# Boundary work between images regrouped, and one of three depthwise-convolution bands computed on VectorE

## The reference

```python
# layer 0
ll, lh, hl, hh = haar(x)                      # four 32x32 bands
q, k, v = heads(qkv_w @ ll)                   # 8 heads of 16, 1024 positions; q, k normalized
attn = softmax(keep_upper_half(q @ k.T / 4))  # each row keeps its 512 largest scores
ll_out = group_norm(proj_w @ (attn @ v))
y = silu(group_norm(depthwise3x3([lh, hl, hh])))      # 384 channels
high = [lh, hl, hh] + alpha * group_norm(pw_w @ y)
out = x + 0.1 * inverse_haar(ll + ll_out, high)
out = out + 0.1 * group_norm(w2 @ gelu(group_norm(w1 @ out)))
# layer 1: full attention over 4096 positions, one head of 16 for q and k
out = gamma * (Wo @ (V @ softmax(Q @ K.T / 4).T)) + out
```

## Time and profile before

| | |
|---|---|
| median of 3 runs | 6547.7 us (6547.65 to 6551.5) |
| profiled execution | 6551.84 us, of which the span of its instructions is 6550.0 us |
| busy share | TensorE 78%, VectorE 69%, ScalarE 70%, GpSimd 6% |
| mean granted TensorE clock | 0.886 |

### The profile page before, as it was taken

One profiled execution on the slowest core, in us unless ns is written; L12 is line 12 of the kernel. 1 busy time (PEld: TensorE's weight loads), 2 busy tenths in 40 slices (PEclk: granted clock), 3 DMA queues, 4 the chain that ended last, 5 costly groups with the idle time before them and its releaser, 6 DMA issues.

```text
span 6550.0 us, 92687 instructions
## 1 busy us (share of the span) xinstructions
PE 5096.8 (78%) x30756; PEld 3132.4 (48%) x30756; DVE 4551.3 (69%) x8207; ACT 4574.2 (70%) x6939; POOL 412.2 (6%) x135
## 2 busy tenths in 40 slices
PE   5343878876888868878788868887688778885788
PEld 2000445653666435553455435664356535563466
DVE  1676479954898469973898559974789649894443
ACT  3885389945998379954999369973799559993223
POOL 3000300011000200012000200003000110000000
PEclk8555889987999879998899879998799879997899
DMA  1001100011000110011000110001100120002000
GB/s 49 6 9 40 51 16 15 14 50 55 13 15 13 56 47 18 16 52 55 9 18 13 48 55 15 18 33 55 28 16 15 50 54 13 16 13 61 9 7 12
DMA packets 109767, 187.72 MB, mean 29 GB/s; under 512 B 48768, under 2 KB 53760, under 8 KB 106144
## 3 DMA queue, kind: packets, MB, share of 16 engines
q1 hardware_dynamic: 109216, 181.05, 9.1%
HBM read 110.61 MB, written 69.47 MB: 27 GB/s over the span
## 4 chain that ended last, share of the span: by engine, by line
DVE 33%; PE 25%; issue 19%; ACT 12%; DMA 5%; SPq 3%; POOL 2%; DVEq 1%; ACTq 0%; POOLq 0%
DVE MX L1400 9%; ACT work L891 7%; PE PS L493 6%; DVE arena L1378 6%; DVE M L1300 5%; PE PS L741 5%; PE PS L462 4%; DVE work L1292 3%; DVE work L1260 3%; DVE work L1284 2%; ACT work L909 2%; PE PS L434 2%; PE PS L405 2%; PE PS L645 2%; PE PS L480 1%
## 5 line engine op out<-in xcount | busy, mean ns | idle before, releaser
L891 ACT ACTIVATE work<-arena,T 128x1024 bf16<-128x1024 f32 x1792 | 2039.7, 1140 | 96.7 <-DVE T L1247 63.9
L493 PEld LDWEIGHTS PS<-V,work 128*128 128x128 f32 x16384 | 2011.1, 194 | 119.8 <-ACT work L916 29.1
L493 PE MATMUL PS<-V,work 128*128 128x129 f32 x16384 | 2040.1, 278 | 22.4 <-ACT work L916 22.4
L1400 DVE TENSOR_REDUCE MX<-PS 128x1 f32<-128x512 f32 x2048 | 1406.4, 687 | 682.8 <-PE PS L462 673.5
L916 ACT ACTIVATE work<-PS 128x1024 f32<-128x1024 f32 x1024 | 1039.6, 1015 | 407.0 <-PE PS L480 406.2
L462 PE MATMUL PS<-KP,QP 96*128 96x512 bf16 x2048 | 854.1, 417 | 511.2 <-DVE MX L1400 388.0
L1378 DVE SCALAR_TENSOR_TENSOR arena<-PS,work 128x1024 f32<-128x1024 f32 x512 | 624.2, 1219 | 260.2 <-ACT work L909 260.2
L462 PEld LDWEIGHTS PS<-KP,QP 96*128 96x128 bf16 x2048 | 201.8, 99 | 1094.3 <-DVE MX L1400 922.4
L881 ACT ACTIVATE arena<-PS 128x1024 f32<-128x1024 f32 x512 | 520.8, 1017 | 264.0 <-PE PS L405 262.9
L480 PE MATMUL PS<-QP,KP 99*128 99x512 bf16 x2048 | 621.1, 385 | 62.6 <-ACT work L916 36.7
L1300 DVE MAX8 M<-work 128x8 f32<-128x1024 f32 x512 | 625.1, 1221 | 3.2
(11 more groups left out here) (176 smaller groups left out, 3858.3 us busy)
## 6 DMA issues: line engine op xcount, KB each, us to landing
work<-scr SPq DMA_DIRECT2D x768, 32.0 KB, 1.8
work<-in_x SPq DMA_DIRECT2D x8, 2048.0 KB, 8.1
arena<-in_x SPq DMA_DIRECT2D x8, 2048.0 KB, 7.9
scrX<-arena SPq DMA_DIRECT2D x8, 2048.0 KB, 6.4
XR<-scrX SPq DMA_DIRECT2D x64, 256.0 KB, 2.7
out<-YO SPq DMA_DIRECT2D x64, 256.0 KB, 2.0
scr<-work SPq DMA_DIRECT2D x24, 512.0 KB, 3.8
scrL<-work SPq DMA_DIRECT2D x24, 512.0 KB, 9.5
```

The source lines that it names most:

```text
L493: last = mm(PS[:, 5 + i // 2, 136 * (i % 2):136 * (i % 2) + 129], P1[:, (16 * j + k) % 3, t, 128 * i:128 * i + 128], V1[:, mt, :], start=( ...
L891: A(JKA[:, m % 2, :], scores(h, i), ACT.Sign, scale=-1.0, bias=T[:, h % 2, i:i + 1], accum_out=CA[:, h % 2, i:i + 1]).then_inc(s["ca"], 1)
L1400: V.reduce_max(MX[:, c % 2, i, w:w + 1], PS[:, 4, :], AX.X).then_inc(s["mr"], 1)
```

## The change

- `NPE = 2`: TensorE convolves two of the three high bands. The third is made on VectorE in nine steps `taps(2, 0)` to `taps(2, 8)`, each over the padded band and, from the second on, the sum so far; GpSimd builds two diagonal weight blocks and not three.
- The wavelet recombination of the finished image (six operations `mix`, four `base`) moves from the start of the boundary into slots 7 and 8. The image is read into XQ, and `add0` writes X1 elsewhere.
- Transfers: the next image comes in two halves, the second after slot 7's search, the first after the last mask; rows of OC and OB of the first seven heads are read before the last head's; a head's queries and keys come by 2 transfers and not 12, from a DRAM layout written by 12 transfers and not 3; QP1 and KP1 come by 7 and not 12; a head's output leaves by 5 and not 8.
- In the boundary `values0` comes first, `qk1` before `values1`, `points` before both; PSUM banks are dealt out anew; on GpSimd `power` of norm 3 comes ahead of `repeat`.
- In the opening slot TensorE makes all eight scores before the first of the 32 `maxima`, and VectorE takes both `centre` steps before it reduces them (`first`).

```diff
+NPE = 2
...
-        DL, GX, GA, GS = arena[:, 4:7, :], arena[:, 7:11, :], units(11, 1), units(14, 1)
-        OC, OB, DL0 = units(12, 1), units(13, 1), units(14, 1)
+        XQ, DL, GA = units(0, 4), arena[:, 4:7, :], units(7, 1)
+        DL0, X1 = units(4, 1), units(12, 4)
+        OC, OB = places(11, 1), places(9, 1)
         HF = units(4, 8).rearrange("p (o n) -> p o n", o=2)
-        F2 = units(12, 4)
+        F2 = HF[:, 1, :]
...
+                done = s["hq%d" % (h % 3)]
+                for w in range(2):
+                    sp.dma_start(QK0[0:KS, h % 3, w, :], scr0[w, h].rearrange("j d n -> (j d) n")).then_inc(done, 16)
...
+            def load_done(b, first):
+                if first:
+                    sp.wait_ge(s["od"], (b * NH + NH - 1) * 80)
+                    rows, heads = slice(0, 112), slice(0, NH - 1)
+                else:
+                    sp.wait_ge(s["od"], (b + 1) * (NH * 80))
+                    rows, heads = slice(112, 128), slice(NH - 1, NH)
+                sp.dma_start(OC[rows], scrO[heads].rearrange("h d n -> (h d) n")).then_inc(s["ol"], 16)
...
+                    if l0 and h == NH - 1:
+                        load_parts(b)
+                    if l0 and h == NH:
+                        load_done(b, True)
+                        if more:
+                            sp.wait_ge(s["p"], (b + 1) * (NH * NT))
+                            sp.sem_inc(s["free"], 1)
+                            load_x(b + 1, 0)
...
+                    if l0 and h == NH - 1 and more:
+                        load_x(b + 1, 1)
...
+                    q, k = scr1[:, 0:16, :], scr1[:, 16:32, :]
+                    for dst, src in ((QP1[0:32], q[0].unsqueeze(0).to_broadcast([2, 16, N1])), (KP1[0:32], k[0:2]),
+                                     (QP1[32:64], q[1].unsqueeze(0).to_broadcast([2, 16, N1])), (KP1[32:64], k[0:2]),
+                                     (QP1[64:96], q[0:3:2]), (KP1[64:80], k[2]), (KP1[80:96], k[0])):
+                        sp.dma_start(dst, src).then_inc(s["qp1"], 16)
...
+                def first():
+                    for i in range(2, NT):
+                        score(0, i)
+                    for k in range(32):
+                        maxima(0, k)
...
+                def mix(h, t):
+                    if not l0 or h != NH - 1:
+                        return
+                    D = [DL[:, o, :] for o in range(3)]
+                    if t == "a":
+                        dve.wait_ge(s["dld"], (b + 1) * 48)
+                        cp.did(V.tensor_tensor(GA, D[2], D[0], ALU.subtract))
...
+                    g = GA if k == 2 else DL[:, 0 if k == 3 else 2, :]
+                    cp.did(V.scalar_tensor_tensor(v, v, 1.2, g.rearrange("p (y x) -> p y x", x=HH), ALU.mult, ALU.add))
+                    made["b%d" % k] = cp.n
...
+                def first():
+                    centre(0, 0)
+                    centre(0, 1)
+                    for k in range(24):
+                        maxima(0, k)
+                        if k in (5, 8, 13, 17):
+                            g = (5, 8, 13, 17).index(k)
+                            update(0, g // 2, g % 2)
...
                     flip(h, 5)
                     maxima(h + 1, 7)
                     eight(h, 5)
+                    mix(h, "a")
                     apart(h, 7)
                     maxima(h + 1, 8)
                     flip(h, 6)
+                    mix(h, "s")
                     maxima(h + 1, 9)
                     eight(h, 6)
+                    mix(h, 0)
                     maxima(h + 1, 10)
                     centre(h + 1, 1)
                     flip(h, 7)
@@ -1498,9 +1589,12 @@
                     match(h)
                     maxima(h + 1, 12)
                     middle(h)
+                    base(h, 0)
                     maxima(h + 1, 13)
                     update(h + 1, 0, 0)
                     threshold(h)
...
                     maxima(h + 1, 17)
                     maxima(h + 1, 18)
                     mask(h, 0)
+                    mix(h, 1)
                     maxima(h + 1, 19)
                     maxima(h + 1, 20)
                     mask(h, 1)
+                    base(h, 1)
                     update(h + 1, 1, 0)
                     maxima(h + 1, 21)
                     update(h + 1, 1, 1)
                     sums(h - 1)
                     maxima(h + 1, 22)
                     mask(h, 2)
+                    mix(h, 3)
                     maxima(h + 1, 23)
+
+                for h in range(-1, NH + 1):
+                    if h == -1:
+                        first()
+                    else:
+                        search(h)
                 cp.wait()
 
 
             def between(f, n, fin, opn):
...
+                def taps(k, t):
+                    if not opn:
+                        return
+                    v = PAD[:, k, t // 3:t // 3 + HH, t % 3:t % 3 + HH]
+                    w = w_dw[:, 9 * k + t:9 * k + t + 1]
+                    o = Y[:, k, :].rearrange("p (y x) -> p y x", x=HH)
+                    if t == 0:
+                        dve.wait_ge(s["pad"], (n + 1) * 3)
+                        ch.did(V.tensor_scalar(o, v, w, None, ALU.mult))
+                    else:
+                        ch.wait(tap[k])
+                        ch.did(V.scalar_tensor_tensor(o, v, w, o, ALU.mult, ALU.add))
+                    tap[k] = ch.n
...
                 norms()
+                power(f, n, fin, opn, 3)
                 repeat()
-                power(f, n, fin, opn, 3)
```

More of the change, by code:

```diff
@@ L306, in slots @@
                         load_rows(a, h)
-                    if l0 and h == NH and more:
-                        load_x(b + 1)
                     if head(h - 1):
@@ L505, in l1_turn, with search @@
                     last.then_inc(s["nt"], 1)
-                for h in range(-1, NH + 1):
+                def first():
[3 more added lines that the diff above has]
+                        maxima(0, k)
+                def search(h):
                     maxima(h, 1)
@@ L821, in between @@
                 group(4)
-                values0(1)
+                points(0, 1)
                 ungroup(4)
-                points(0, 1)
                 points(1, 0)
+                points(1, 1)
+                points(2, 0)
+                points(2, 1)
+                qk1()
+                group(2)
                 values1(0)
                 values1(1)
+                ungroup(2)
                 values1(2)
@@ L831, in between @@
                 values1(5)
-                qk1()
                 values1(6)
                 values1(7)
-                points(1, 1)
-                points(2, 0)
-                points(2, 1)
-                group(2)
-                ungroup(2)
             pe.wait_ge(s["w"], 16 * 12)
@@ L1125, in between @@
                 ffn1(2)
+                ffn1(3)
+                ffn1(4)
                 qk0(3)
[L1127 to L1130 removed]
                 ffn1(5)
                 ffn1(6)
[L1133 removed]
+                square(3)
                 ffn1(7)
@@ L1443, in slots @@
                     mask(h - 1, 4)
+                    base(h - 1, 3)
+                    based(h - 1)
                     update(h, 2, 0)
@@ L1503, in slots @@
                     threshold(h)
+                    mix(h, 2)
+                    base(h, 2)
                     maxima(h + 1, 14)
@@ L1712, in between @@
                 moments(0)
-                base(2)
-                mix(3)
                 variance(0)
-                base(3)
                 scales(0)
@@ L1728, in between @@
                 ffn1(4)
+                taps(2, 0)
+                ffn1(5)
+                conv(0, 0)
+                taps(2, 1)
+                taps(2, 2)
                 clamp()
-                ffn1(5)
+                taps(2, 3)
+                taps(2, 4)
                 ffn1(6)
+                taps(2, 5)
                 ffn1(7)
+                taps(2, 6)
+                conv(0, 1)
                 ffn1(8)
@@ L1740, in between @@
                 ffn1(13)
+                taps(2, 7)
                 ffn1(14)
@@ L1743, in between @@
                 moments(3)
+                taps(2, 8)
+                variance(3)
+                conv(1, 0)
+                scales(3)
+                conv(1, 1)
                 conv(2, 0)
-                variance(3)
-                scales(3)
                 normal(0)
@@ L1925, in _ @@
             pool.wait_ge(s["dset"], DSET)
-            for k in range(3):
+            for k in range(NPE):
                 TT(diag[:, 9 * k:9 * k + 9, :], ident.unsqueeze(1).to_broadcast([128, 9, 128]),
```

426 lines of the change are left out of this document (204 added, 222 removed).

## The result

The changed kernel takes 6581.79 us (median of 5 runs, 6576.83 to 6584.36), the kernel before 6547.76 (6547.65 to 6551.5): a ratio of 1.0048, 95% interval 1.0036 to 1.0060. The forecast was 6492, range 6355 to 6550. The profiled execution takes 6579.38 us, with a span of 6577.6 against 6550.0, +27.6.

A forecast was written before the change was run, and what follows sets the result against it. Image boundaries, 221.8 us each, were taken to hold nearly all of the change. Per boundary +2.2 - 7.7 = -5.5, seven times -38, first -8, last -10: -56, so 6551.8 becomes 6496, or 6492 at the median; range 6355 to 6550.

The forecast's parts named there:

- KP should be there: Opening slot: KP lands by the end of centre at +48, its loads starting near +30 and taking half as long.
- The taps and the power: VectorE during norms: a tap waits 20.8 us for GpSimd's power, so all that TensorE gained is gone.
- rival 1: During norms: GpSimd's power does not hold VectorE back for its length; -24 us a boundary, 6355 in all; chance 0.15.
- first score: Between the last ffn2 and the next search: first score 28.8 us after the last ffn2, 39.5 before.
- first count: Opening slot: first count behind 24 maxima comes 80.6 us after the last ffn2, against 88.3 before.
- The first boundary: Boundary that only opens: one diagonal block less, squares some 4 us earlier, same power wait; -8 us (0 to -14).
- The last: Last boundary, without norms: qk1 no longer behind six values1, wider loads in the 22 us wait; -10 us (-3 to -14).
- slot 7's threshold: End of the search on VectorE: four recombination operations ahead of it make it 4.5 us later.
- `add0`: Start of the boundary: done 3.5 us earlier, between 1 and 6, at 2198.3 against 2201.8.
- rival 2: Dense stretch after the idle 17 us: TensorE's clock stays low, say +15 us a boundary, 6597 in all; chance 0.10.
- Rival 3: Whole change does not do what it says: transfers or mixes cost what the tail gains, 6535 to 6560; chance 0.09.
- the tail: From the last ffn2 to the next search's first count: 7.7 us less per boundary.

The follow-up runs named there:

- e9: Six extra GpSimd additions ahead of its power, so that VectorE's taps run beside additions, added to the kernel of e7; 0.2% over the kernel before, 6563.1 us.
- e7: The kernel of e5 with the twelve head-plane stores laid out with 128 rows outermost, not 8 heads; 6404.5 us.
- e2: The changed kernel with QP1 and KP1 filled by twelve loads of 16 rows, and PT1's three stores split into twelve of 32 rows; 6432.0 us.
- e5: The kernel of e2 with the 2 MB store into scrX issued behind the loads of QP1 and KP1; 6409.6 us.
- e10: The kernel of e7 with scr1 and its transfers as in the kernel before (three stores of 128 rows, twelve loads); 6390.1 us.
- e3: The kernel of e2 with the old opening order, maxima and scores alternating after two scores; 6445.9 us.
- e12: The kernel of e11 with the old opening order, maxima and scores alternating after two scores; 6340.4 us.
- e11: The kernel of e10 with the 16 rows of each QP1 and KP1 load six partitions apart, not side by side; 6387.9 us.

## Why the prediction was wrong

The sign was wrong, by two errors that partly cancelled. The step that turned the sign is the second: "KP should be there".

1. "**The taps and the power**": "I take 20.8". No tap waits for the power; the power waits 1.0 us for a tap. This was rival 1's mechanism (0.15), and its size was right too: gelu forecast near 242 and the last ffn2 at 2264.4 in old time, 16.4 gained; measured 14.6. The rows I argued from had additions of GpSimd (L1855, L1871) as partners, and I carried them over to a power. e9 shows the reading of the additions to be right, whole instructions and all, and the carrying over to be the error. The sentence that I put beside it from the Trainium skill (SBUF — State Buffer, "Who interferes with whom"), that whoever is first holds the pair for the whole instruction, agrees with the additions of e9 and is not what the trace shows for the power: taps start and end inside its 21.8 us.
2. "**KP should be there**: its loads start near +30 ... seven on mostly 32 should take half". Counted from the last ffn2, the first store of PT1 is issued at +24.5 and the first load at +41.8, not near +30: 17.3 us lie between them (2279.06 to 2296.34), where it was 9.7, as 11.4 lie there in the last boundary, where it was 3.4. The stores use four engines. Then the loads take 30 us to the first `maxima` and not 11, twice the 14.6 us of the twelve before, because five of the seven use two engines. The new opening order puts the scores ahead of the wait, so it hides 17 us of it; the rest is the 20.22. The other part of that sum held where it can be seen alone: first score at +34.5 (forecast +28.8), of which 6.0 is an unnamed wait, so the products ended at +28.5. In e7, where KP is in time, the boundary after image 0, without that unnamed wait, has the first score at +28.3 and its first count at +79.5 (forecast +80.6). Here it is +105.0 (before +88.3).
3. "**The first boundary ... -8 (0 to -14)**": measured -9.4 at the first score, so this term was right. No tap of the run waits (the longest of 64 takes 1.36 us), and this boundary loads no KP.
4. "**The last ... wider loads in the 22 us wait; I take -10**": measured +22.4: -3.2 ahead of the first store of PT1, +23.0 the transfers, +2.6 behind the first `maxima`.
5. Right: slot 7's threshold 3.7 us later (forecast 4.5); `add0` 3 us earlier (3.5); slots at 66.94; no wait for DL in slot 7; granted clock 1.00 in the ffn2 stretch, so rival 2 did not happen. The mean granted clock is 0.874 (0.886 before); the longer waits behind that stretch, where windows show 0.50, are a likely reason.

Per ordinary boundary: -14.6 + 16.7 is +2.1, and the chain shows +2.15. The text's own list of what would show it wrong named both ("taps of 1.2 us during `norms`", "TensorE waiting for KP after the scores"), but priced only the first. Rival 3 had the second as 0.09, and never below what the tail gains.

One term was missing from the tail: TensorE's wait ahead of the first score, which the profile files under "issue". Of all its waits of the run:

```profile
PE PS L428 <- issue: 31.2, 5, 6.4
```

It comes five times and not seven. The kernel runs images 1 to 6 in a loop, and the five are the boundaries after which TensorE jumps back to the loop's head. After images 0 and 6, where it does not jump, the first score follows `values1` at once and stands 28.3 us after the last ffn2. In the wait after image 2 (2283 to 2289) the DMA view shows four instruction transfers among the stores, two of 16 KB and two of 8 KB. The wait is 7.08 us in e2 and 3.68 in e5, where the 2 MB of scrX come later. That the jump makes TensorE wait for its own instructions, and that other traffic lengthens this, fits all of it, but it is not shown: no run took the loop away. The kernel before has the wait too (3.49 in the earlier trace rows), inside the 39.5 us that I read there.

What stays open: why the power does not hold a tap, and where the ten us of e10's 14 lie that are not in the last boundary.

## What to carry to other kernels

Count engines before bytes: look first at the outermost loop of each side of a transfer, on which the number of working engines hung here, and then at which partitions they reach; seven larger loads took twice as long as twelve smaller ones. A wait seen between two instructions is evidence for that pair of operations only; when a forecast hangs on another pair, say that it is carried over and give the other outcome its full weight. An order of issue has no value of its own: e3 and e12 are the same edit with opposite signs, decided by when one buffer lands.

## What the runs showed of the hardware

- Transfers with an outermost loop of 2, 4 or 8 moved 52, about 100 and 200 GB/s (shares 0.13, 0.26, 0.53), those of 128 rows 380 (share 1.00).
- Sixteen full engines moved only 112 to 146 GB/s into 16 neighbouring partitions, and 197 at a share of 0.67 with the same rows six partitions apart (e10 and e11). The Trainium skill says that bandwidth depends on how many ports the partitions reach (SBUF — State Buffer, "Door 1: The DMA port swizzle"); the trace agrees.
- GpSimd's power of 128x128 lasts 20.8 us, and VectorE's operations with two SBUF operands run beside it at 1.27 us. Beside GpSimd's additions of 128x1024 they take 2.76 to 3.25 us and end 1.1 us after the addition; the addition takes 3.2 to 3.3 us instead of 2.36.
- Ahead of its first product behind a jump back to the head of its loop TensorE stood 6.0 us in the kernel after (7.1 in e2, and 3.7 in e5, where 2 MB of stores come later). Where it did not jump it did not stand.
